# The last expert's result in quarters, x back in eight loads, and layer 2 started on the moments of four tiles

## The reference, cut to what matters

```python
# layer 1, mixture of 8 experts: each takes the CAP = 512 tokens with its highest gate
tok = tok.at[idx_flat].add(y.reshape(-1, d))        # y = gate * expert(layernorm(tok[idx]))
return tok.reshape(x.shape)

# layer 2
x = x + g_msa * _attention(_modulate(_layernorm(x), sh_msa, sc_msa), W_qkv, W_out, b_out)
x = x + g_mlp * _ff(_modulate(_layernorm(x), sh_mlp, sc_mlp), W1, b1, W2, b2)
```

## Time and profile before

| | |
|---|---|
| median of 3 runs | 3171.31 us (3167.34 to 3174.15) |
| the profiled execution: its span | 3174.1 us |
| run with that time in the list | 3174.15 us |
| handoff from the last expert to layer 2: PE idle | 39.1 us |
| attention of layer 2: L746 of tile 0 to L746 of tile 31 | 1586.1 to 2191.6 us |
| granted TensorE clock, mean | 0.949 |

### The profile page before, as it was taken

How to read it: one execution, slowest core, us unless ns; L and a number is a source line. 1 busy time by engine, 2 the same in 40 slices (tenths; PEclk the granted TensorE clock), 3 DMA queues, 4 the chain that set the end, 5 groups by cost and what they waited for, 6 DMA issues and landing times.

```text
span 3174.1 us, 68515 instructions
## 1 busy us (share of the span) xinstructions
PE 2816.6 (89%) x27492; PEld 2035.9 (64%) x27492; DVE 1718.0 (54%) x4184; ACT 915.7 (29%) x1646; POOL 332.9 (10%) x390
## 2 busy tenths in 40 slices
PE   6999789999999922899499999998998898989999
PEld 6888656666666621566488888885444777755555
DVE  4666667777777656432344444443333788852221
ACT  1333245555555500112122222222111233321110
POOL 0111101101010000232111111110000111100000
PEclk9999889999999955999799999998999899989999
DMA  5000000000000030343300000000000000000000
GB/s 183 0 0 0 4 21 20 26 20 26 23 23 26 14 116 7 103 106 83 113 0 0 0 0 0 0 0 1 1 0 1 0 0 0 0 1 14 14 14 14
DMA packets 62245, 77.36 MB, mean 24 GB/s; under 512 B 12577, under 2 KB 52001, under 8 KB 61665
## 3 DMA queue, kind: packets, MB, share of 16 engines
q1 hardware_dynamic: 56032, 67.88, 6.4%
q0 software_dynamic: 6144, 8.52, 1.4%
HBM read 59.33 MB, written 17.06 MB: 24 GB/s over the span
## 4 chain that ended last, share of the span: by engine, by line
PE 53%; DVE 30%; issue 9%; ACT 4%; DVEq 2%; DMA 1%; POOL 0%; SPq 0%; ACTq 0%; POOLq 0%
PE psS L1052 7%; PE psW L293 6%; PE psW L286 5%; DVE work L634 5%; PE psP L463 4%; PE psP L1025 4%; PE psP L1019 4%; PE psS L1046 4%; PE psO L1019 3%; PE psO L1025 3%; DVE work L636 2%; PE psO L408 2%; PE psP L455 2%; PE psO L326 2%; PE psP L392 2%
## 5 line engine op out<-in xcount | busy, mean ns | idle before, releaser
L293 PE MATMUL psW<-r,work 128*128 128x512 f32 (+1 forms) x1280 | 556.5, 566 | 6.0 <-DVE work L671 3.7
L286 PE MATMUL psW<-work,r 128*128 128x128 f32 x3072 | 385.6, 284 | 14.8 <-DVE work L623 9.1
L286 PEld LDWEIGHTS psW<-work,r 128*128 128x128 f32 x3072 | 364.7, 197 | 33.4 <-DVE work L623 21.9
L904 ACT ACTIVATE work<-work 128x512 f32<-128x512 f32 x256 | 161.2, 630 | 621.2 <-DVE work L636 621.2
L293 PEld LDWEIGHTS psW<-r,work 128*128 128x128 f32 x1280 | 224.8, 191 | 175.6 <-issue 150.0
L952 POOL TENSOR_TENSOR work<-work 128x512 f32<-128x512 f32 x128 | 130.8, 1043 | 1280.8 <-DVE work L645 1280.8
L1052 PE MATMUL psS<-r,work 128*128 128x256 f32 x1024 | 225.3, 381 | 6.1 <-DVE work L1122 5.3
L1052 PEld LDWEIGHTS psS<-r,work 128*128 128x128 f32 x1024 | 193.2, 190 | 36.0 <-DVE work L1122 6.1
L392 PE MATMUL psP<-consts,work 128*128 128x128 f32 x1024 | 152.7, 284 | 54.7 <-ACT work L904 49.1
L636 DVE TENSOR_TENSOR work<-psS,work 128x512 f32<-128x512 f32 x256 | 177.1, 692 | 16.3
L634 DVE TENSOR_REDUCE work<-psS 128x8 f32<-128x512 f32 x256 | 175.0, 683 | 7.7 <-PE psS L372 5.1
(11 more groups left out here) (191 smaller groups left out, 4231.7 us busy)
## 6 DMA issues: line engine op xcount, KB each, us to landing
r<-in_l_fc SPq DMA_DIRECT2D x16, 1024.0 KB
work<-mod_rows SPq DMA_DIRECT2D x64, 128.0 KB, 2.8
r<-in_l_w SPq DMA_DIRECT2D x2, 3072.0 KB, 13.3
x<-in_x SPq DMA_DIRECT2D x4, 1024.0 KB, 12.5
gather_table<-work SPq DMA_DIRECT2D x32, 128.0 KB, 1.8
moe_sum<-work SPq DMA_DIRECT2D x32, 128.0 KB, 1.7
x<-moe_sum SPq DMA_DIRECT2D x4, 1024.0 KB, 9.5
out<-x SPq DMA_DIRECT2D x8, 512.0 KB, 2.9
```

Source lines behind the costliest of these rows:

```text
L286: ins = nc.tensor.matmul(ps[:, q * P:(q + 1) * P], w[:, k, lo + q * P:lo + (q + 1) * P], L.hT[:, k, :], start=(k == 0), stop=(k == KC - 1))
L293: ins = nc.tensor.matmul(ps[:, 0:width], L.hT[:, k, :], w[:, k, lo:lo + width], start=(k == 0), stop=(k == KC - 1))
L904: nc.scalar.activation(E, E, ACT.Exp, scale=scale).then_inc(L.s[f"exp{i}"].sem, 1)
```

## The change

Five things are changed.

1. For the last expert alone, PE writes each quarter of the result to a bank of its own and signals it. DVE adds the bias and multiplies by the gate quarter by quarter (two instructions of 128x256 each), and POOL issues each indirect transfer as soon as its quarter is done.
2. x comes back in eight loads of 4 tiles.
3. DVE's first step of layer 2 takes the moments of tiles 0 to 3 and the reciprocal root of those four columns alone.
4. The moments of the later groups of four tiles are computed in the steps of layer 2: those of group t/4+1 at the end of step t when t is 0, 4, ..., 24, and their reciprocal root at the end of step t when t is 1, 5, ..., 25. Both stand behind `dve_l2_y`.
5. DVE's steps of layer 2 are written out, all 32, with the tile number as a constant; the other engines keep their loop.

```diff
+        def dve_back_group(v, ch, i):
+            v.wait_ge(ld[f"back{i}"], 16)
+            dve_group_moments(ch, i)
+
+        def dve_back_rstd(ch, i):
+            dve_rsqrt(ch, rstd[:, 4 * i:4 * i + 4], moments[:, 4 * i:4 * i + 4, 1])
...
+                elif L.li == 2:
+                    dve_back_group(v, ch, 0)
+                    dve_back_rstd(ch, 0)
                 else:
                     dve_rstd(ch, rms=L.li == 3)
...
                     dve_l2_y(v, ch, L, t)
+                    if t % 4 == 0 and t // 4 + 1 < NT // 4:
+                        dve_back_group(v, ch, t // 4 + 1)
+                    if t % 4 == 1 and t // 4 + 1 < NT // 4:
+                        dve_back_rstd(ch, t // 4 + 1)
...
+            if L.li == 2:
+                first()
+                for t in range(NT):
+                    step(t, min(3, NT - 1 - t), t > 0)
+                last()
+                return
             tiles(v, NT, first, step, last)
...
+        LAST = [psS[:, 0:D], psS[:, 512:512 + D], psP[:, 0:D], psP[:, 512:512 + D]]
...
+                if is_last_expert(Q, t):
+                    for r in range(4):
+                        for j in range(FJ):
+                            ins = nc.tensor.matmul(LAST[r], Q.hid[:, j, r * P:(r + 1) * P],
+                                                   Q.w2[u][:, j, :], start=(j == 0), stop=(j == FJ - 1))
+                        ins.then_inc(Q.s["f_y"].sem if r == 3 else lastx["y"], 1)
+                    return
...
+                if is_last_expert(Q, t):
+                    for r in range(4):
+                        if r < 3:
+                            v.wait_ge(lastx["y"], r + 1)
+                        else:
+                            after(v, Q.s["f_y"], t + 1)
+                        if r == 0:
+                            after(v, Q.s["f_sc"], t * 64)
+                        ch.link(nc.vector.tensor_tensor(Q.y[:, r, :], LAST[r], Q.b2[u], ALU.add))
+                        ins = nc.vector.tensor_scalar(Q.y[:, r, :], Q.y[:, r, :], Q.wcol[u][:, r:r + 1], None, ALU.mult)
+                        ins.then_inc(Q.s["f_done"].sem if r == 3 else lastx["done"], 1)
+                    return
...
                 for r in range(4):
+                    if is_last_expert(Q, t):
+                        if r < 3:
+                            g.wait_ge(lastx["done"], r + 1)
+                        else:
+                            after(g, Q.s["f_done"], t + 1)
                     nc.gpsimd.indirect_dma_start(
...
-            for i in range(4):
-                sp.dma_start(x[:, 8 * i:8 * i + 8, :], by_tile(moe_sum)[:, 8 * i:8 * i + 8, :]
+            for i in range(8):
+                sp.dma_start(x[:, 4 * i:4 * i + 4, :], by_tile(moe_sum)[:, 4 * i:4 * i + 4, :]
                              ).then_inc(ld[f"back{i}"], 16)
...
-            dve_all_moments(v, ch, [ld[f"back{i}"] for i in range(4)])
             dve_attention(v, ch, L[2])
```

More of the change, by code:

```diff
@@ L218, in build_program @@
         slot_token = nc.dram_tensor("slot_token", [E8 * CAP], I32, kind="Internal").ap()
-        ld = sems("ld", "small m0 m1 m2 m3a m3b x0 x1 x2 x3 back0 back1 back2 back3 l0 l1 l2 l3 rows")
+        ld = sems("ld", "small m0 m1 m2 m3a m3b x0 x1 x2 x3 back0 back1 back2 back3 back4 back5 back6 back7 l0 l1 l2 l3 rows")
         st = sems("st", "out tab gates idx rows")
@@ L995, in __init__, with is_last_expert @@
                     self.s |= signals("f_gi0 f_gi1 f_si0 f_si1", NG // 2 * 16)
+        LAST = [psS[:, 0:D], psS[:, 512:512 + D], psP[:, 0:D], psP[:, 512:512 + D]]
+        def is_last_expert(Q, t):
+            return Q.kind == "moe" and isinstance(t, int) and t == NG - 1
         HB = [psP[:, 0:512], psP[:, 512:1024], psO[:, 0:512], psO[:, 512:1024]]
@@ L1216, in step @@
                     gather(t + 2, u, half + 1)
-                after_all(g, su["table"], [(Q.s[f"f_si{u}"], (half + 1) * 16), (Q.s["f_done"], t + 1),
-                                           (Q.s["f_sc"], t * 64)])
-                for r in range(4):
+                if is_last_expert(Q, t):
+                    after_all(g, su["table"], [(Q.s[f"f_si{u}"], (half + 1) * 16), (Q.s["f_sc"], t * 64)])
+                else:
+                    after_all(g, su["table"], [(Q.s[f"f_si{u}"], (half + 1) * 16), (Q.s["f_done"], t + 1),
+                                               (Q.s["f_sc"], t * 64)])
+                for r in range(4):
+                    if is_last_expert(Q, t):
+                        if r < 3:
+                            g.wait_ge(lastx["done"], r + 1)
+                        else:
+                            after(g, Q.s["f_done"], t + 1)
                     nc.gpsimd.indirect_dma_start(
@@ L1381, in build_program @@
         hotAt = W.take(GE * 8).bitcast(BF16).rearrange("p (t n) -> p t n", n=P)
+        lastx = sems("lastx", "y done")
         rt = sems("rt", "shift exp prob cnt tot keep cnt2 tot2 m w hot ix idx")
```

## The result

The changed kernel takes 3177.91 us (median of 12 runs, 3176.61 to 3179.81) against 3171.59 us (12 runs of the kernel before, 3167.34 to 3175.45). The quotient of these medians is 1.0020; the ratio on record is 1.0027, with a 95% interval of 1.0019 to 1.0034. So the change makes the kernel slower, by about the 0.2% that can just be told from no change. Forecast were 3179.6 us and "slower" with a chance of 0.56. One execution each in the experiments on the written-out steps (3810.53 us) and without the quarters (8806.98 us) ran at a far lower clock and is left out of their figures.

The account below looks back on a forecast made before the run. PE, busy 89% of the span, was taken as the bound. Handoff -23.4, written-out steps -17.6, moved work +35.8 and clock +13.5 gave +8.3 us, so 3171.3 becomes 3179.6 us, range 3165 to 3191.

Parts of the forecast that it names:

- Handoff: PE's pause between the last expert and layer 2: quarters, smaller loads, fewer moments and a smaller root gain 23.4 us.
- Quarters: At the handoff, sending the last expert's result in quarters lets SP issue the loads of x 7.2 us earlier.
- POOL's lag: At the handoff, POOL's time from the last quarter being ready to its scatter, taken as 0.84 us; bound 0.30.
- The eight loads: At the handoff, a first load of x of half the size lands 1.45 us earlier.
- Moments and root: DVE's start of layer 2: one group of moments instead of eight saves 14.5 us, the smaller root 0.3.
- Written-out steps: DVE's steps in layer 2: without register work 27 tiles gain 0.64 us each, the first about half; 17.6 us.
- the row over the page: For layer 2's written-out steps, the trace's 0.64 us per tile was preferred to the skill page's 0.108 us.
- Moved work: Layer 2: seven groups of moments and seven roots, inserted outside DVE's idle time, are paid in full, 35.8 us.
- The clock: Layer 2: pauses of PE at insertions lower its clock, nine falls of 1.5 us each, +13.5 us.
- The clock stays high: Rival, chance 0.35: layer 2's new pauses leave the clock wholly or mostly high; 3166.1 us, up to 3177.
- Partly hidden: Rival, chance 0.09: clock stays and layer 2's insertions partly hide behind PE's queued work; faster, 3152 to 3165 us.
- the written-out steps bring nothing: Rival, chance 0.08: PE's and ACT's loops or program fetching set layer 2's tile; slower, 3197 us.

## Why the prediction was right, point by point

**Handoff.** Forecast 23.4, measured 39.09 - 14.58 = 24.5 us. Quarters: forecast 7.2, measured 7.9 against the kernel before and 7.7 in the experiment without them. The term that was off is POOL's lag: taken as 0.84 us, it was 0.28 (1511.63 to 1511.91), near the bound of 0.30. The 0.84 us belonged to the first of the four scatters: in the changed kernel, too, the first quarter's takes 0.79 us (1501.27 to 1502.06). The eight loads: 1.45 forecast from the bandwidth rows, 1.46 in the experiment (1.7 against the kernel before). Moments and root: 14.8 forecast, 14.9 measured.

**Written-out steps.** Forecast 17.6, measured 20.0. The tile fell to 18.96, not to 19.02 us, which is 0.70 to 0.71 for 27 tiles, and the first and the last interval gained 0.4 and 0.5. The 0.108 us per tile of the Trainium skill (Advanced Engine Details and Errata, section Control Flow Timing) is for the compare-and-branch alone. In the loop's trace 0.19 us lie between the start of the branch and the next instruction, a smaller part of the 0.70 us; the rest went at places where the loop has register instructions ahead of waits and addresses. No run takes the two apart. The choice for the row over the page was right.

**Moved work.** Forecast 35.8 in full, none hidden. Measured: 7 x 2.10 for the moments, 7 x 3.10 for the roots without the clock, 36.4 us. That all of it is paid because of where it stands is shown by the kernel in which it stands ahead of the output. The pauses were read off rightly, too: 1.75 and 2.75 forecast, 1.70 and 2.65 measured.

**The clock.** The mechanism was right, the term too large. Nine falls of 1.5 us were forecast, 13.5; it was seven, one behind every root and none behind moments, four at 1.25 us and three at 1.0 to 1.2. That makes 8.2 us, which is also what is left of the 44.6 us that layer 2 holds above the written-out kernel, less 36.4. The size of a fall was taken from the rate of L286 at both levels over the whole stretch, and L286 does lose 1.62 us there (5.46 instead of 3.84). Of this 0.37 us are given back later in the tile. One place is the second L286: in the tiles with moments its weights wait 0.30 us for ACT's L861, in those with a root not at all. The rest was not traced. The Trainium skill (TensorE: Matmul & The Clock Gate, section Loop structure matters more than you think) says that DVE's copy of a result between two groups of matmuls does not break PE's warmth; it speaks of matmuls that follow immediately and gives no length. Taken as a rule for any pause that DVE makes, it held here for the pauses of 1.70 us and less and failed for 2.65.

**Layer 3.** Not forecast: +2.7 us from the position of an untouched loop. With it the sum of the traces is -24.5 - 20.0 + 36.4 + 8.2 + 2.7 = +2.8 us. So by the traces the forecast of +8.3 was 5.5 too high: the clock term by 5.3 and the gains of handoff and steps by 3.5 on one side, the moved work by 0.6 and layer 3 by 2.7 on the other. The medians say +6.3, so that the forecast fits them to 1.7 us is in part luck. The traces' sum agrees with their spans: these differ by 1.9 us, and the changed kernel's execution was 1.2 us ahead when the last expert ended. The 3.5 us between this sum and the medians stay open, and the sum lies below the interval on record, which is 6.0 to 10.8 us. One execution of each kernel was traced. Unchanged stages before the handoff differ by up to 3.9 us between executions, and the last interval of layer 2 by about 2 us, as shown above.

**The rivals.** "The clock stays high" has fallen in the changed kernel and describes the version with the split root. "Partly hidden" and "the written-out steps bring nothing" have fallen.

## What to carry to other kernels

Work moved into a pipeline belongs into the idle time of its engine, and that time has a definite place in the engine's order: here the same 36 us of work cost 45 us, the clock included, behind the instruction that waits, and nothing that the tiles show ahead of it. Look in the timeline for the instruction that carries the idle time, and put the work before it. Before a loop on an engine that is on the chain is left as it is, compare its tile with the steps written out at its end: where they are shorter, the difference is what the loop may cost. Here it was 0.64 us seen there and 0.70 us gained.

## What the runs showed of the hardware that was not expected

- Writing out DVE's steps alone took 0.70 us off a 19.66 us tile while every other engine kept its loop, and 1.1 us off layer 3's (10.82 to 9.72).
- The same loop of layer 3, unchanged, takes 10.60, 10.70, 10.72 or 10.82 us per tile, depending on what stands before it in DVE's program; DVE is idle for 0.24, 0.34, 0.36 or 0.46 us at its turn. A change elsewhere can thus cost or gain up to 6 us in this kernel.
- Inside layer 2, PE's pauses of 1.06, 1.24 and 1.70 us (1.77 in the two kernels with added instructions) left the clock at 2.4 GHz, every time. Each of 2.65 us (2.72 there) was followed by a stretch at 1.2 GHz, 35 times in five kernels. It lasted 3.4 us and cost up to 1.25 us; in four of these kernels one of the seven lasted 6.8 us, and its tile 24.6 to 24.7 us.
